# Releasing the indirect gathers one at a time in a recommendation tower kernel

## The reference, cut to what matters

```python
e = jnp.stack([tbl_0[ids[:, 0]], ..., tbl_15[ids[:, 15]]], axis=1)
A = jnp.repeat(x0, s, axis=1)
Bm = jnp.repeat(xl, f, axis=2).reshape(b, s * f, d)
z = jnp.einsum('bnh,bnd,nk,khd,kd->bkh', A, Bm, alpha, w, hv[..., 0])   # x0 = e, xl = r_x0
h = jnp.concatenate([z.reshape(b, -1), dense_ctx], axis=1)
h = jnp.maximum(h @ W_top1 + b_top1, 0.0)      # 272 x 512
h = jnp.maximum(h @ W_top2 + b_top2, 0.0)      # 512 x 256
y = h @ W_top3                                 # 256 x 1
```

## Time and profile before

| what | value |
|---|---|
| device time, median of 3 (lowest to highest) | 196.21 us (194.47 to 199.51) |
| profiled execution, span from first to last instruction | 296.9 us |
| PE busy, share of the span, instructions | 226.7 us, 76%, 2630 |
| DVE busy | 153.7 us, 52%, 173 |
| POOL busy | 116.6 us, 39%, 120 |
| ACT busy | 76.1 us, 26%, 212 |
| DMA moved | 32.72 MB, mean 110 GB/s |

### The profile page before, as it was taken

The page is one execution under the profiler, slowest core; times in us unless marked ns, Lnnn a source line. Parts: engine busy times, 40 slices in busy tenths (PEclk is TensorE's granted clock), DMA queues, the critical chain, the costliest instruction groups (busy, mean ns, idle before and its releaser), DMA issues.

```text
span 296.9 us, 6045 instructions
## 1 busy us (share of the span) xinstructions
PE 226.7 (76%) x2630; PEld 156.7 (53%) x2630; DVE 153.7 (52%) x173; ACT 76.1 (26%) x212; POOL 116.6 (39%) x120
## 2 busy tenths in 40 slices
PE   6221676989698569969692989889697796699996
PEld 2200564447377328646451866657466564347774
DVE  5500291086869349544480494929628673066900
ACT  3500350271422140306000350314023022022322
POOL 4777017100636361723446034634561737400000
PEclk9999995559779897968897797979759997569999
DMA  6976205000779715640255046460544334000000
GB/s 180 258 168 188 121 2 121 2 3 3 183 264 304 273 10 143 223 151 2 59 116 205 0 146 148 139 234 6 147 149 145 78 76 148 6 2 0 2 0 2
DMA packets 14579, 32.72 MB, mean 110 GB/s; under 512 B 6499, under 2 KB 10448, under 8 KB 11472
## 3 DMA queue, kind: packets, MB, share of 16 engines
q1 hardware_dynamic: 9717, 29.95, 32.4%
q0 software_dynamic: 3712, 0.96, 3.3%
q10 hardware_dynamic: 1124, 1.43, 1.6%
HBM read 32.28 MB, written 0.05 MB: 109 GB/s over the span
## 4 chain that ended last, share of the span: by engine, by line
PE 49%; another core or an unknown queue 14%; issue 7%; ACT 4%; DVE 0%; ACTq 0%
PE bank L773 14%; PE bank L706 10%; PE bank L700 9%; PE bank L728 8%; PE bank L761 3%; PE bank L693 3%; ACT tower L546 2%; ACT e_cols L569 1%; PE bank L714 1%; PE bank L752 1%; PE bank L686 0%; ACT tower L548 0%; ACT ids_b L540 0%; ACT tower L602 0%
## 5 line engine op out<-in xcount | busy, mean ns | idle before, releaser
L420 POOL DMA_INDIRECT e<-tbl_dram,ids_all x116 | 116.4, 1003 | 139.9 <-DVE prod L509 104.2
L509 DVE TENSOR_TENSOR prod<-x,bank 128x2048 f32<-128x2048 f32 x40 | 91.2, 2283 | 59.9 <-issue 30.5
L437 DVE TENSOR_SCALAR onehot<-ids_b 125x2304 bf16<-125x2304 f16 (+5 forms) x90 | 51.5, 621 | 21.4 <-PE bank L728 20.3
L728 PE MATMUL bank<-parts,onehot 125*128 125x48 bf16 x1248 | 45.6, 189 | 22.2 <-issue 20.4
L728 PEld LDWEIGHTS bank<-parts,onehot 125*128 125x128 bf16 x1248 | 40.6, 100 | 31.4 <-issue 27.2
L773 PE MATMUL bank<-prod,m_w 128*32 128x256 f32 x640 | 52.4, 431 | 4.6 <-issue 3.6
L700 PE MATMUL bank<-tower,w_z 128*128 128x256 f32 x128 | 39.5, 457 | 6.0 <-ACT tower L602 5.6
L706 PE MATMUL bank<-tower,w 128*128 128x256 f32 x128 | 36.9, 429 | 6.2 <-ACT tower L546 4.5
L773 PEld LDWEIGHTS bank<-prod,m_w 128*32 128x32 f32 x640 | 22.0, 122 | 27.2 <-issue 20.1
L700 PEld LDWEIGHTS bank<-tower,w_z 128*128 128x128 f32 x128 | 27.4, 226 | 14.4 <-ACT tower L602 8.3
L706 PEld LDWEIGHTS bank<-tower,w 128*128 128x128 f32 x128 | 26.7, 220 | 13.7 <-ACT tower L546 6.6
(11 more groups left out here) (47 smaller groups left out, 86.9 us busy)
## 6 DMA issues: line engine op xcount, KB each, us to landing
x<-x_dram SPq DMA_DIRECT2D x16, 1024.0 KB
x<-x_dram SPq DMA_DIRECT2D x16, 512.0 KB
ids_b<-ids_half_dram SPq DMA_DIRECT2D x4, 576.0 KB
e<-tbl_dram,ids_all POOLq DMA_INDIRECT x116
prod<-windows_c_dram ACTq DMA_DIRECT2D x1, 768.0 KB
prod<-windows_c_dram ACTq DMA_DIRECT2D x1, 512.0 KB
w_z<-w_z_dram SPq DMA_DIRECT2D x1, 512.0 KB
w<-w_dram SPq DMA_DIRECT2D x1, 512.0 KB
```

The costliest lines, as they stand in the source:

```text
L420: nc.gpsimd.indirect_dma_start(out=e[:, tile, f * D:(f + 1) * D], out_offset=None, in_=t[f"tbl_{f}"][:, :], in_offset=bass.IndirectOffsetO ...
L437: nc.vector.tensor_scalar(onehot[:, at % NPLANE, lo:hi, :], ids_b[0:TP, n % 2, lo:hi, :], float(k), None, ALU.is_equal).then_inc(hot_made, 1)
L509: nc.vector.tensor_tensor(prod[:, s % NPROD, :].rearrange("p (q b) -> p q b", q=HP), x0[:, tile % NX, :].rearrange("p (q b) -> p q b", q=H ...
L728: made = nc.tensor.matmul(out, onehot[:, PLANE_AT[n, lo, k] % NPLANE, j, bt * P:(bt + 1) * P], parts[:, KT_AT[f] + k, :, :], start=k == 0 ...
```

## The change

Each gather now waits by itself, on one engine's count. From half 1 on, the gathers of half n are dealt out over the five steps of half n - 1: 2, 3, 3, 3, 3 of them (3, 4, 3, 4, 4 for half 7). In a step the first goes when the product is made, the second when the step's first plane is made, the third (and a fourth) when its last plane is made; a step without planes lets all go with its product. In half 0 the first six still go at once, the next two when TensorE has summed two blocks of alpha, and the last six when all five are summed, and then behind the 3rd, 6th, 10th, 13th and 16th plane that TensorE has picked from.

```diff
+def _beside():
+    found = {}
+    for n in range(1, NH):
+        of_half = sum(2 * len(fs) for fs in GATHERED[n])
+        for g in range(UH):
+            s = UH * (n - 1) + g
+            planes = [PLANE_AT[n_hot, lo, k] + 1 for n_hot, lo, hi, k in PLANES.get(s, [])]
+            marks = [("prod", s + 1)] + ([("hot", planes[0]), ("hot", planes[-1])] if planes else [("prod", s + 1)] * 2)
+            for i in range(g * of_half // UH, (g + 1) * of_half // UH):
+                found[n, i] = marks[min(i - g * of_half // UH, 2)]
+    return found
+
+BESIDE = _beside()
+
+FRONT_AB = {6: 2, 8: FT}
+FRONT_HOT = {9: 3, 10: 6, 11: FIRST_PLANES, 12: FIRST_PLANES + 3, 13: FIRST_PLANES + 6}
...
-GATHERS_AFTER = [-1, 1, 2]
...
+                at = 0
                 for j in range(3):
-                    if UH * (n - 1) + GATHERS_AFTER[j] > 0:
-                        pool.wait_ge(prod_made, UH * (n - 1) + GATHERS_AFTER[j])
                     for f in GATHERED[n][j]:
                         for tile in range(2 * n, 2 * n + 2):
+                            if n == 0 and at in FRONT_AB:
+                                pool.wait_ge(ab_summed, FRONT_AB[at])
+                            elif n == 0 and at in FRONT_HOT:
+                                pool.wait_ge(hot_used, FRONT_HOT[at])
+                            elif n > 0 and BESIDE[n, at][0] == "prod":
+                                pool.wait_ge(prod_made, BESIDE[n, at][1])
+                            elif n > 0:
+                                pool.wait_ge(hot_made, BESIDE[n, at][1])
                             nc.gpsimd.indirect_dma_start(
...
+                            at += 1
```

## The result

| what | before | after |
|---|---|---|
| device time, median | 196.16 us (4 runs, 194.47 to 199.51) | 205.72 us (4 runs, 204.8 to 208.69) |
| profiled execution, span | 296.9 us | 203.5 us |
| its device time | not shown | 205.38 us |

The ratio is 1.049, 95% interval 1.0446 to 1.0535: the change makes the kernel slower by some 9.5 us. The range of 192 to 204 missed it.

The account below looks back on a forecast made before the run. TensorE was taken to bound the timed run, with 162 to 188 us of work in 196.21 us. Half 7 added 2.0 us and all else 0, so 196.2 + 2.0 = 198 us (+1.0%), range 192 to 204.

Parts of the forecast that it names:

- the term of half 7: Last half: all 18 gathers leave from product 30's end, fill 2 is 0.7 to 2.9 us late; 2.0 taken, bounds 0 and 4.
- A landing of 0.9 us: Half 7's last gather: time from its issue to its data's arrival, taken as 0.9 us from traffic with the queues idle.
- it fits, by 0.15 us: POOL's rate in each step: three gathers take 3.75 us against a step of 3.9 us on TensorE.
- merely runs on: POOL, if planes stretch its gathers: it falls a little behind its marks and continues as now, at no cost.
- an unmet wait: Waits on about 110 gathers: one not yet met lets go 0.26 us after the product, a met one costs nothing.
- a gather's pace: Gathers on POOL: each takes 0.94 + 0.30 = 1.25 us when alone.
- planes beside gathers: Steps with planes: VectorE pays 0.01 us a pair, 0.3 us over 30 steps, hidden; POOL pays 0.35 a gather.
- The port rule of the Trainium skill: VectorE and GpSimd share an exclusive port lock, so gathers block planes; 28 us, 224 if VectorE is on the path; chance 0.03.
- The front: Half 0's held gathers delay loads by some 5 us; between no loss and 1.3 us, no loss taken.
- Group 0 of halves 3 to 6: Its sixth gather leaves four products later but lands in time, but for 0.9 us at worst; cost taken as 0.
- Rival (b): Group 0 lands late in every half and TensorE waits for fill 0; 5.5 us plus half 7, 204 us; chance 0.21.
- Rival (a): Pauses beside trains of gathers are in timed runs too; some 7 us won, half 7 costs 1.5, 191 us; chance 0.15.

Follow-up runs that it names:

- e5_half7: The kernel before with only half 7's gathers dealt out as in the change, front and halves 1 to 6 as before; 203.52 us, ratio 1.0271 to before.
- e16_earlier: The changed kernel with every mark of halves 2 to 7 two steps earlier, front still held; 196.76 us, ratio 1.0045 to the kernel before.

## Why the prediction was wrong

**The step that failed is the term of half 7**: "Fill 2 is 0.7 to 2.9 us late ... I take 2.0", with bounds 0 and 4. The late fill, its place and its sign were right. The size was not, 6.7 us at the end of the kernel, and it lies outside the bounds because three pieces were wrong: when POOL is free, how long a landing takes, and a clock cost that the sum did not have. Piece by piece, in us; T is the end of product 30, 154.24 after and 156.19 in e5_half7:

| | predicted | measured after | e5_half7 |
|---|---|---|---|
| POOL starts 18 gathers | T + 0.26 | T + 1.46 | T + 0.27 |
| last gather issued | T + 22.5 | T + 23.7 | T + 22.7 |
| ScalarE has its data | T + 23.4 | T + 25.2 | T + 24.3 |
| TensorE asks | T + 21.4 to 23.6 | T + 21.8 | T + 21.8 |
| TensorE waits | 0.7 to 2.9 | 4.48 | 3.56 |
| half clock behind it | not in the sum | 2.1 | 1.7 |

TensorE's time to ask is its resumption less its wait: 180.54 - 4.48 = 176.06, and 181.58 - 3.56 = 178.02. It lies in the range worked out from the earlier trace rows, near the low end, where I took the middle. A landing of 0.9 us was the traffic's end without what follows to ScalarE; 1.6 us are measured twice. POOL's late start is "it fits, by 0.15 us" failing. The steps are not of one length, and the two ahead of half 7 are the short ones. Products 28, 29 and 30, then the first gathers of steps 28 and 29:

```profile
145.43 2.27 DVE L533 TENSOR_TENSOR prod<-x,bank 128x2048 f32<-128x2048 f32 x1
148.69 2.27 DVE L533 TENSOR_TENSOR prod<-x,bank 128x2048 f32<-128x2048 f32 x1
151.97 2.27 DVE L533 TENSOR_TENSOR prod<-x,bank 128x2048 f32<-128x2048 f32 x1
```

```profile
147.97 1.09 POOL L443 DMA_INDIRECT e<-tbl_dram,ids_all  x1 [0.40 <-DVE prod L533]
...
151.93 0.94 POOL L443 DMA_INDIRECT e<-tbl_dram,ids_all  x1 [0.30 <-issue]
```

The gather at 147.97 is on time, 0.27 us after product 28. Six gathers then take 155.70 - 147.97 = 7.73 us, and the two steps give 6.54 (151.97 - 145.43), where the prediction had 3.9 for each. That is the 1.2 us by which POOL is late; gathers stretched beside planes make up 0.2 of it (7.73 against 6 x 1.25). The sentence that POOL "merely runs on" left out that half 7 then starts later. And the clock was left out altogether, though the earlier trace rows had warned of it: a wait of 3.5 to 4.5 us on a TensorE that is otherwise full was followed by a layer at about half speed.

**Right:** an unmet wait adds 0.26 us and a met one nothing; a gather's pace is 1.25 us here too; planes beside gathers cost VectorE nothing measurable (e16_earlier at 1.0045). The port rule of the Trainium skill (SBUF — State Buffer, SBUF: two separate sides), a rival at 224 us, is not seen on VectorE. The Trainium skill has it there for a VectorE instruction in a two-port mode, and no run shows the mode of the planes. In the changed kernel 35 of the 48 planes of 125x2304 started while a gather was under way, and their median is 0.75 us, that of the two planes with no gather beside them. It is GpSimd's gather that takes longer. A gather of the changed kernel and the planes beside it, of POOL and of DVE:

```profile
130.58 1.28 POOL L443 DMA_INDIRECT e<-tbl_dram,ids_all  x1 [0.30 <-issue]
```

```profile
131.00 1.42 DVE L461 TENSOR_SCALAR onehot<-ids_b 125x2304 bf16<-125x2304 f16 x2
```

The gather began first and took 1.28 us instead of 0.94; the pair of planes took the usual 1.42. The front is free within 1%, again by e16_earlier, which contains it.

**Group 0 of halves 3 to 6,** taken as 0: ScalarE does wait, up to 5.0 us, with landings of up to 7.1 us from a gather's start, where the longest taken was 0.94 + 4.8 = 5.7. But of TensorE's waits for fills only the 0.69 us of half 5 belong here, and 1.11 us to half 2, for whose group 0 the prediction had no term. The 1.17 us in the front stand in e16_earlier too, as its only such wait:

```profile
PE bank L785 <- ACT e_cols L593: 1.2, 1, 1.2
```

The cover, ScalarE's and TensorE's own order, held for the most part. Rival (b), which would have put 5.5 us here, is refuted as the main cause.

**Rival (a)** had the right observation and the wrong reading, as had I. The stutter is in timed runs, but in all of them of some places and none of others. The sum of TensorE's work against 196 us was a sound argument that the timed runs of before were free of it, though the 18.6 us were a stretch that also holds 22 records; its pauses add up to some 14 us. In the stuttering places dealing out the gathers gains 2 to 6%.

**What stays open.** The difference of medians is 205.6 - 196.8 = 8.8 us and the end accounts for 6.7. By the two ratios, 1.046 and 1.0045, the difference is 8 us, uncertain by some 2, so what is left over is hardly clear of noise. It may be the 1.8 us of TensorE's waits for fill 0, but from product 5 to product 30 the profiled executions of the changed kernel and of e16_earlier need 96.4 and 96.0 us (151.97 - 55.59, 151.66 - 55.65), so their profiles don't show it. Over all seven profiles of quick places this stretch takes 95.7 to 98.6 us, too wide a spread for 1.8 us. No run moved half 7's marks alone to two steps earlier. Why some places stutter was not found out: their records show only pauses named "issue" while gathers leave in a train. No profile of the kernel before was had in a quick place; e5_half7 is the same as it up to the end of product 28, when the kernel before lets half 7's first gathers go.

## What to carry to other kernels

Spreading transfers "over the previous stage" fixes their earliest start: before doing so, multiply the count of the largest stage by the time of one issue and lay it against the time until its last consumer asks. Here 18 x 1.25 + 1.6 + 0.9 = 25 us stood against 21.8, and marks two steps earlier gave it back to within 1%. Take the length of the very steps ahead of that stage, not their average: 3.3 us against 3.9 made POOL 1.2 us late. An in-order queue passes lateness on: putting back only the last group's marks helped nothing. A wait on an engine without slack can cost more than its length: here 4.5 us of wait were 6.7 us.

And hold a profile's span against the timed median before reading any pause in it: here the two differ by 100 us, as the same kernel does from chip to chip.

## What had not been expected of the hardware

- The same kernel takes 193 to 202 us on some chips and 279 to 309 on others. There TensorE runs in bursts of a few instructions with pauses of 0.4 to 1.5 us while gathers leave back to back.
- A gather of 128 rows of 64 bytes takes 3.2 us in the median from the start of its issue to its landing and up to 7.1, in a kernel that loads 1 MB tiles beside it, though its issue takes 0.94.
- After a wait of 4.48 us the granted clock fell, and eight records took 3.62 us instead of 1.89. Idle transposes up to 1.16 us ahead of the next work kept it up.
